# Second attention of a fused block: scaled float16 pairs in place of float32 operands

## What is computed

```python
q = jnp.einsum('btm,mhd->bthd', x, w_aq)
k = jnp.einsum('btm,mhd->bthd', x, w_ak)
v = jnp.einsum('btm,mhd->bthd', x, w_av)
q = _rope(q)
k = _rope(k)
s = jnp.einsum('bihd,bjhd->bhij', q, k) / D_HEAD
...
s = s - jnp.asarray(INF_APPROX, x.dtype) * mask
p = jax.nn.softmax(s, axis=-1)
o = jnp.einsum('bhij,bjhd->bihd', p, v)
r = jnp.einsum('bihd,hdm->bim', o, w_ao)
```

## Time and profile before

| | |
|---|---|
| median of 3 runs | 2135.99 us (2134.03 to 2136.79) |
| the profiled execution | 2136.71 us, its span 2134.9 us |
| attention A's loop | from 58 us, 1212 us long |
| attention B's loop | from 1376.7 us, 711.6 us long |
| mean granted clock of TensorE | 0.978 |

### The profile page before, as it was taken

One profiled execution on the slowest core, in us unless ns is written; L12 is line 12 of the kernel. 1 busy time (PEld: TensorE's weight loads), 2 busy tenths in 40 slices (PEclk: granted clock), 3 DMA queues, 4 the chain that ended last, 5 costly groups with the idle time before them and its releaser, 6 DMA issues.

```text
span 2134.9 us, 51602 instructions
## 1 busy us (share of the span) xinstructions
PE 1976.8 (93%) x21751; PEld 1427.7 (67%) x21751; DVE 1522.4 (71%) x2818; ACT 1478.4 (69%) x1812; POOL 1280.5 (60%) x687
## 2 busy tenths in 40 slices
PE   4899999999999999999999987699999999999997
PEld 3466666656666666666666655478788887878886
DVE  7777777877777777787777756666666766667642
ACT  2788888888888888888888983245555454554563
POOL 5798898898888988988988981222313122131200
PEclk8999999999999999999999998699999999999999
DMA  5100100110110010010011001000000000000000
GB/s 134 31 15 18 31 17 17 32 24 10 32 31 13 20 32 17 17 31 22 14 29 31 2 2 50 1 1 1 1 1 1 1 1 1 1 1 1 1 1 20
DMA packets 45013, 37.67 MB, mean 18 GB/s; under 512 B 8304, under 2 KB 44144, under 8 KB 44528
## 3 DMA queue, kind: packets, MB, share of 16 engines
q1 hardware_dynamic: 43824, 33.60, 6.4%
q10 hardware_dynamic: 960, 0.79, 0.2%
HBM read 8.15 MB, written 1.05 MB: 4 GB/s over the span
## 4 chain that ended last, share of the span: by engine, by line
PE 79%; DVE 16%; issue 2%; ACT 1%; POOL 1%; ACTq 0%; DMA 0%; SPq 0%; DVEq 0%
PE ST L1354 9%; PE ST L1355 9%; PE OO L1491 7%; PE RING L1229 6%; PE OO L1298 5%; PE OO L1300 5%; PE OO L1297 5%; DVE maxes L903 4%; PE RING L1444 3%; PE OO L1229 3%; PE ST L1514 3%; PE ST L1491 3%; PE ST L1518 3%; PE ST L1516 3%; PE RING L1424 3%
## 5 line engine op out<-in xcount | busy, mean ns | idle before, releaser
L517 POOL TENSOR_TENSOR PAB<-PR,PAB 128x1024 f16<-128x1024 f32 x342 | 724.2, 2132 | 98.0 <-ACT PAB L655 96.2
L903 DVE TENSOR_REDUCE maxes<-RING 128x1 f32<-128x512 f32 x710 | 468.8, 684 | 148.3 <-PE RING L1229 147.8
L655 ACT ACTIVATE PAB<-ST,exp_scale 128x1024 f16<-128x1024 f32 x512 | 567.2, 1108 | 0.0
L653 ACT ACTIVATE PR<-ST,exp_scale 128x1024 f32<-128x1024 f32 x342 | 381.3, 1115 | 123.6 <-PE ST L1355 120.1
L1297 PE MATMUL OO<-VP,PAB 128*128 128x66 f16 x4096 | 440.4, 193 | 2.8 <-POOL PAB L517 2.8
L1298 PE MATMUL OO<-VP,PAB 128*128 128x64 f16 x4096 | 441.0, 194 | 0.0
L1300 PE MATMUL OO<-VP,PAB 128*128 128x66 f16 x4096 | 438.7, 192 | 0.0
L1297 PEld LDWEIGHTS OO<-VP,PAB 128*128 128x128 f16 x4096 | 379.6, 96 | 73.0 <-issue 15.7
L1298 PEld LDWEIGHTS OO<-VP,PAB 128*128 128x128 f16 x4096 | 376.9, 97 | 60.2
L1354 PE MATMUL ST<-QL,KH 128*128 128x512 f16 x1024 | 388.5, 379 | 2.3 <-ACT PAB L655 1.4
L517 POOL TENSOR_TENSOR PAB<-VF,PAB 128x1024 f16<-128x1024 f32 x170 | 362.5, 2132 | 44.4 <-ACT PAB L655 43.3
(11 more groups left out here) (202 smaller groups left out, 3260.8 us busy)
## 6 DMA issues: line engine op xcount, KB each, us to landing
KH<-HS SPq DMA_DIRECT2D x120, 64.0 KB, 2.0
QL<-HS SPq DMA_DIRECT2D x64, 64.0 KB, 2.0
QL<-LS SPq DMA_DIRECT2D x64, 64.0 KB, 2.0
QH<-HS SPq DMA_DIRECT2D x64, 64.0 KB, 2.0
KL<-LS SPq DMA_DIRECT2D x60, 64.0 KB, 2.0
X<-in_L_attn_a_x SPq DMA_DIRECT2D x4, 256.0 KB, 4.8
SHARED<-in_rope_cos SPq DMA_DIRECT2D x1, 1024.0 KB, 4.8
SHARED<-in_rope_sin SPq DMA_DIRECT2D x1, 1024.0 KB, 7.6
```

Of the source, the lines that this page charges most:

```text
L517: pool.tensor_tensor(PB[:, s, :], PRA[g % PR_SLOTS], PA[:, s, :], ALU.subtract).then_inc(p_low_ready, 1)
L653: act.activation(PRA[g % PR_SLOTS], ST[step % 2][:, :], ACT.Exp, scale=scale)
L655: act.activation(PA[:, step % SLOTS_A, :], ST[step % 2][:, :], ACT.Exp, scale=scale).then_inc(sa.exps, 1)
L903: dve.reduce_max(maxes[:, i // BLOCKS, i % BLOCKS:i % BLOCKS + 1], bank[:, :], X_AXIS).then_inc(sa.ring_taken, 1)
```

## The change

Attention B gets float16 pairs throughout.

- **Weights.** During attention A ACT squares the weights of B, DVE sums them, one product totals them (ring item `total`), and DVE makes a power of two of each head's Q, K and V from the exponent. POOL multiplies the weights by it in 12 pieces, ACT writes the high halves (WHB) and POOL the low halves (WLB).
- **x.** XNT is replaced by XH and XL: ACT writes the high part of a transposed block, DVE the low part.
- **Projections and values.** Each is three products (high·high, low·high, high·low). ACT writes the high part of V and DVE the low part. V is laid out as two columns of ones, 128 high, 128 low.
- **Scores.** Four products add up: `row_units` (4 rows of 2^15) times MROW (the scaled negative maximum of each query, one row for each query tile), then the three products of K and Q in float16; on the diagonal the mask product too. `spread`, its copy, the priming and the fill go, and scores(g) waits for the exps of step g - 2 alone.
- **P.** ACT takes exp twice from PSUM: into float32 (PRB, three slots) and into float16 (PAH, four slots). POOL subtracts (PAL). P·V of step g is three products a query tile and follows the scores of step g + 2.
- **Order.** Projections and values sit at other steps. POOL does the rope sum one step after the projection and the low part of Q or K four steps after; ACT does the high part three steps after. DVE normalises a unit at step 2 of the next. The first two score steps stand ahead of the eight maxima of the second unit.

```diff
+LAG_B = 2
+SLOTS_B = 4
+PR_SLOTS_B = 3
+PIECES_B = 12
...
-VALUES_B = {(2, 4): 0, (2, 7): 1, (2, 10): 2, (3, 9): 3}
-PROJECT_B = {(1, 5): [0], (2, 3): [1], (2, 6): [2], (2, 9): [3], (3, 1): [4], (3, 3): [5], (3, 5): [6], (3, 8): [7]}
+VALUES_B = {(2, 1): 0, (2, 11): 1, (3, 9): 2, (3, 12): 3}
+PROJECT_B = {(1, 1): [0], (1, 4): [1], (1, 7): [2], (2, 3): [3], (2, 6): [4], (2, 9): [5], (3, 1): [6], (3, 5): [7]}
...
-    if step == steps_b(qb) - 3 and (next_qb or next_head):
-        items += [("spread", next_qb)]
...
+                i = u - UNITS_A
+                if 0 <= i < PIECES_B and step == 0:
+                    pool.wait_ge(b_scaled, 1)
+                    wait(pool, wb_high, i - 1)
+                    pool.tensor_tensor(wb_tmp[:, i % 2, :, :],
+                                       RAW[:, i * 2 * DB:(i + 1) * 2 * DB].rearrange("p (a c) -> p a c", c=DB),
+                                       b_up[:, 2 * i:2 * i + 2].unsqueeze(2).broadcast_to((P, 2, DB)), ALU.mult
+                                       ).then_inc(wb_put, 1)
+                if 0 <= i < PIECES_B and step == 4:
+                    pool.wait_ge(wb_high, i + 1)
+                    pool.tensor_tensor(piece_b(WLB, i), wb_tmp[:, i % 2, :, :], piece_b(WHB, i), ALU.subtract
+                                       ).then_inc(wb_low, 1)
...
-                high, low = ((QH, QL), (KH, KL))[j % 2]
+                high, low = ((QH16, QL16), (KH16, KL16))[j % 2]
                 pool.wait_ge(sbb.high_ready, index + 1)
-                pool.tensor_tensor(low[hs][:, q], F[:, j % 2, :], high[hs][:, q].bitcast(F32),
-                                   ALU.subtract).then_inc(sbb.operands_ready, 1)
+                pool.tensor_tensor(low[hs][:, q], F[:, j % 2, :], high[hs][:, q], ALU.subtract
+                                   ).then_inc(sbb.operands_ready, 1)
 
...
+            for g, (it, ul, step) in enumerate(PLACES_B):
+                c0 = max(0, step - BT * (ul % BLOCKS)) * P
+                pool.wait_ge(sbb.exps, g + 1)
+                wait(pool, sbb.pv, g - SLOTS_B + 1)
+                pool.tensor_tensor(PAL[:, g % SLOTS_B, c0:BLK], PRB[g % PR_SLOTS_B][:, c0:BLK],
+                                   PAH[:, g % SLOTS_B, c0:BLK], ALU.subtract).then_inc(p_low_ready_b, 1)
+                for head, n, j in projects_before(g, 1):
+                    rope_sum_b(j, n)
+                for head, n, j in projects_before(g, 4):
+                    low_b((head + 1) % 2, j, (head + 1) * 2 * BLOCKS + j)
 
...
                                ).then_inc(sa.exps, 1)
+                if u == 1 and step in (1, 3, 5):
+                    act.wait_ge(bweights, 48)
+                    part = slice(step // 2 * 8 * DB, (step // 2 + 1) * 8 * DB)
+                    act.activation(PBUF[:, part], RAW[:, part], ACT.Square, scale=float(np.sqrt(D))
+                                   ).then_inc(b_squared, 1)
+                i = u - UNITS_A
+                if 0 <= i < PIECES_B and step == 2:
+                    act.wait_ge(wb_put, i + 1)
+                    act.activation(piece_b(WHB, i), wb_tmp[:, i % 2, :, :], ACT.Copy).then_inc(wb_high, 1)
...
+            for g, (it, ul, step) in enumerate(PLACES_B):
+                hs, qb = divmod(ul, BLOCKS)
+                head = it * 2 + hs
+                c0 = max(0, step - BT * qb) * P
+                scale = exp_scale_b[:, head:head + 1]
+                wait(act, p_low_ready_b, g - PR_SLOTS_B + 1)
+                act.wait_ge(sbb.scores, g + 1)
+                act.activation(PRB[g % PR_SLOTS_B][:, c0:BLK], SB[g % 2][:, c0:BLK], ACT.Exp, scale=scale)
+                wait(act, sbb.pv, g - SLOTS_B + 1)
+                act.activation(PAH[:, g % SLOTS_B, c0:BLK], SB[g % 2][:, c0:BLK], ACT.Exp, scale=scale
+                               ).then_inc(sbb.exps, 1)
+                for n, item in ITEMS_B[g]:
+                    if item[0] == "values":
+                        values_high_b(1 - hs, item[1], RING[n % 2], n)
+                for phead, n, j in projects_before(g, 3):
...
                 q = slice(b * BLK, (b + 1) * BLK)
-                dve.tensor_tensor(XL[:, q], O[b % 2][:, :], XH[:, q], ALU.subtract).then_inc(xnt_ready, 1)
+                dve.tensor_tensor(XL[:, q], bank[:, :], XH[:, q], ALU.subtract).then_inc(xnt_ready, 1)
 
...
-                    link(dve.tensor_copy(negparts[:, 0:BT].bitcast(F32R), negmax[:, :]))
-                    dve.tensor_tensor(negparts[:, BT:AUX], negmax[:, :], negparts[:, 0:BT],
-                                      ALU.subtract).then_inc(s.max_ready, 1)
+                    dve.tensor_scalar(negparts[:, :], negmax[:, :], 1.0 / ROW_UNIT, lifts_b[:, head:head + 1],
...
+            def take_values_b(hs, part, bank, item, count):
+
+                dve.wait_ge(vb_high, count)
+                v = VBS[:, hs, part * BT:(part + 1) * BT, :]
+                dve.tensor_tensor(v[:, :, V2B_AT:VB], bank[:, :].rearrange("p (t c) -> p t c", c=DB),
+                                  v[:, :, V1B_AT:V2B_AT], ALU.subtract).then_inc(sbb.ring_taken, 1)
...
+            for g, (it, ul, step) in enumerate(PLACES_B):
+                hs, qb = divmod(ul, BLOCKS)
+                head = it * 2 + hs
+                if step == LAG_B and g > step:
+                    normalise_b((ul - 1) % UNITS_B, g - step)
...
-            def project_b(hs, j, bank, item, head):
+            def project_b(j, bank, item, head):
 
                 claim(sbb, item)
-                pe.wait_ge(sbb.wst_ready, head + 1)
-                blk = j // 2
-                pe.matmul(bank[:, :], WST[:, hs, (j % 2) * DB:(j % 2 + 1) * DB], XNT[:, blk * BLK:(blk + 1) * BLK],
-                          start=True, stop=True).then_inc(sbb.ring_put, 1)
-
-            def values_b(hs, part, bank, item, head):
+                pe.wait_ge(wb_low, PIECES_B)
+                q = slice(j // 2 * BLK, (j // 2 + 1) * BLK)
+                w = slice(j % 2 * DB, (j % 2 + 1) * DB)
+                pe.matmul(bank[:, :], WHB[:, head, w], XH[:, q], start=True, stop=False)
+                pe.matmul(bank[:, :], WLB[:, head, w], XH[:, q], start=False, stop=False)
...
+            def scores_b(g):
+
+                it, ul, step = PLACES_B[g]
+                hs, qb = divmod(ul, BLOCKS)
+                if step == 0:
+                    pe.wait_ge(sbb.ring_taken, ROWS_OF_B[it * UNITS_B + ul] + 1)
+                wait(pe, sbb.exps, g - 1)
+                keys = slice(step * P, (step + 1) * P)
+                c0 = max(0, step - BT * qb) * P
+                q = slice(qb * BLK + c0, (qb + 1) * BLK)
+                tile = SB[g % 2][:, c0:BLK]
+                pe.matmul(tile, row_units[:, :], MROW[:, qb % 2, c0:BLK], start=True, stop=False,
+                          skip_group_check=True)
+                if step >= BT * qb:
+                    pe.matmul(SB[g % 2][:, c0:c0 + P], mask_ident[:, :], later_keys_t[:, :], start=False,
+                              stop=False, skip_group_check=True)
+                pe.matmul(tile, KH16[hs][:, keys], QH16[hs][:, q], start=False, stop=False, skip_group_check=True)
+                pe.matmul(tile, KL16[hs][:, keys], QH16[hs][:, q], start=False, stop=False, skip_group_check=True)
+                pe.matmul(tile, KH16[hs][:, keys], QL16[hs][:, q], start=False, stop=True, skip_group_check=True
+                          ).then_inc(sbb.scores, 1)
+
...
+            def pv_b(g, half):
...
-                    pe.wait_ge(sbb.exps, g + 1)
+                    if step == 0:
+                        pe.wait_ge(sbb.ring_taken, VALUES_OF_B[it * 2 + hs] + 1)
+                        wait(pe, sbb.o_taken, it * UNITS_B + ul - 1)
+                    pe.wait_ge(p_low_ready_b, g + 1)
+                v = VBS[:, hs, step, :]
                 for qt in range(max(2 * half, step - BT * qb), 2 * half + 2):
-                    bank, at = (OB[ul % 2][0], qt * VB) if qt < 3 else (OB[ul % 2][1], 0)
-                    ins = pe.matmul(bank[:, at:at + VB], PRB[:, step % 2, qt * P:(qt + 1) * P],
-                                    VBS[:, ul // BLOCKS, step, :], start=(step == 0 and qt in (0, 3)),
-                                    stop=(step == BT * qb + qt), skip_group_check=True)
+                    bank, at = (OB[ul % 2][0], qt * V2B_AT) if qt < 3 else (OB[ul % 2][1], 0)
+                    o = bank[:, at:at + V2B_AT]
+                    tile = slice(qt * P, (qt + 1) * P)
+                    high, low = PAH[:, g % SLOTS_B, tile], PAL[:, g % SLOTS_B, tile]
+                    pe.matmul(o, high, v[:, 0:V2B_AT], start=(step == 0 and qt in (0, 3)), stop=False,
+                              skip_group_check=True)
+                    pe.matmul(o[:, V1B_AT:V2B_AT], high, v[:, V2B_AT:VB], start=False, stop=False,
+                              skip_group_check=True)
+                    ins = pe.matmul(o, low, v[:, 0:V2B_AT], start=False, stop=(step == BT * qb + qt),
...
+            for g, (it, ul, step) in enumerate(PLACES_B):
...
```

(16 more changed lines are left out.)

518 lines of the change are left out of this document (230 added, 288 removed).

## The result

| | before | after |
|---|---|---|
| median of 4 runs, us | 2136.4 (2134.0 to 2136.8) | 2230.6 (2229.4 to 2232.1) |
| profiled span, us | 2134.9 | 2229.6 |
| first attention, first score product to end | 58.5 to 1269.3 | 61.3 to 1284.4 |
| second attention's loop | 711.6 | 792.5 |
| a head of it | 91.1 | 99.9 to 103.1 |

The account below looks back on a forecast made before the run. PE was taken to bound the second attention. Heads of 76.5 + 7 = 83.5 us made its loop 650, 61.5 less; with +5, -0.5, -2.5 and +0.5 that is -59 from 2136.0: 2077 us, range 2042 to 2112.

Parts of the forecast that it names:

- PE's work a head, 76.5: Second attention: PE's products, priced by columns, sum to 75.4 us a head; 76.5 taken, 10.7 less than before.
- Waits, 7 (4 to 12): Second attention: PE's new waits a head; those listed come to 10 us, 7 taken, 4 and 12 as bounds.
- The maximum behind a projection: Block rows 1 and 2: PE reaches maxima behind DVE's projections too early, by 0.85, 0.5, 0.85 and 0.4 us.
- The turn: Block rows 1 to 3: PE waits at the turn for DVE, 1.4, 1.3 and 1.7 us.
- (f): Scaled negative maximum on DVE takes 0.23 to 1.59 us; PE waits 0.4 at the rows product; worst case 38 over the stage.
- POOL (e): Second attention: a rope sum or low part on POOL delays P's low part, needed for P·V; 1.3 us a head.
- First attention, +5 (0 to +12): First attention: added ACT, POOL and DVE work on the weights costs 5 us, between 0 and 12.
- between -2.5: Between the attentions: spread, priming and first fill go, low parts of X come; -2.5 us, between +3 and -6.
- A: Second attention: waits stay at 4 us a head as in the first; head 80.5, time 2048; chance 0.24.
- B: Second attention: P's low part comes late from POOL, 9.7 us more waits a head; 2110 (2103 to 2122); chance 0.15.
- C: Second attention: every projection's 2.07 us on DVE is exposed, 16.6 a head; time 2144; chance 0.08.
- D: Second attention: each 130-column P·V instruction holds PE for 0.10 us, 18 more a head; time 2221; chance 0.03.

Follow-up runs that it names:

- e1_rows128: The changed kernel with 128 rows, 124 of them zeros, instead of 4 in the product that brings the maximum in; 2177.4 us.
- e10_new_places_rows4: The kernel with the best order found (e5_new_places), with the 4-row product put back; 2124.1 us against 2062.7.
- e5_new_places: The changed kernel with the 128-row product, the output's own wait, and projections, values, turn, output, rope sums and high parts at other steps; 2062.7 us.
- e4_output_own_wait: The 128-row kernel with turn and output one step later in rows 1 to 3, its output waiting only for its turned tile's copy; 2124.5 us.
- e9_rows64: The changed kernel with 64 rows instead of 4 in the product that brings the maximum in; 2220.9 us, one run.
- e3_old_places: The 128-row kernel (e1_rows128) with values and projections at the steps of the kernel before; 2162.4 us.
- e8: e5_new_places with three-operand scaled maximum, later start fills, sums and exponent arithmetic spread over units, GpSimd's weight pieces at step 4; 2048.3 us.

## Why the prediction was wrong, step by step

The prediction is off by 154 us. Two terms of its sum failed. "Four float16 products (three pairs and the new product of rows) cost 4 x 7.36 = 29.5 us" priced the product of rows by its columns; it costs 61 us more. And "A head takes 76.5 + 7 = 83.5" had the waits too small and gave no price to what comes with them: with 128 rows and the order unchanged (e1_rows128) a head takes 95.0, 11.5 over my 83.5, some 90 us over the loop. Either would have spoiled the forecast: without the first the kernel still takes 2177, and without the second it takes 2124 (e10_new_places_rows4). By its own steps:

- **PE's work a head, 76.5: right but for one term.** In e5_new_places, at a clock of 1.00 and with 128 rows, PE works for 76.6 (my 1.5% on top of the 75.4 is an allowance that no run takes apart). Float16 P·V at 0.057, scores at 0.216, the diagonal, the projections: each as priced. The failed term is that of the scores, four products at one price: the fourth has four rows and costs 0.192 more a step, 7.7 a head, 61.4 in all. I had the evidence and did not use it: the four spreads of 512 columns that the change removes stand in my sum at "some 1.5", 0.38 each where columns give 0.22. They have 8 rows. Two rows of the kernel before, PE's timeline in its second attention:

```profile
1465.28 0.49 PE L1473 MATMUL RING<-MROW,ones_r 8*128 8x512 f32 x1
1465.70 0.71 PE L1491 MATMUL OO<-PAB,PR 128*128 128x129 f32 x4
```

  The successor starts 0.42 behind the 8-row product, 0.20 later than its columns ask for. (That its rows cost this, and not its format, wasn't tested.) I took that price away with the spreads, four a head, and did not put it on the 40 products of rows that come.
- **Waits, 7 (4 to 12): 10.9 by the waits view, inside the bounds, but not the waits I listed; 13.5, outside them, once the rows cost nothing (e1_rows128).** The maximum behind a projection: 2.6 forecast, 3.0 seen. The turn: 1.4, 1.3 and 1.7 forecast, 2.6 seen. The rows product (f): 0.4 forecast, 1.35 seen (12.7 over the loop, where my worst case was 38). POOL (e): 1.3 forecast, none seen for P·V; POOL's lateness shows at DVE instead, 3.7 once a head, for the buffer F, and some 1.4 of it at PE, within the 3.0 at maxima. Not in my list at all: the output, 3.2. I had costed the moved places and not the order of items within a step nor the argument of the wait that the diff drops; e4_output_own_wait puts that wait, with what came along, at 31 us.
- **What a wait costs.** From e1_rows128 to e5_new_places the order alone takes 115 us away. A head in the middle of the loop falls by 17.1, from 95.0 to 77.85, and the waits in it by 12.4, from 13.5 to 1.1. The rest has two parts. First, a wait breaks PE's stream: the product ahead of it shows its whole length, 0.38 where the next one would start after 0.22 in a stream, or 0.22 where it would start after 0.06. So each wait takes some 0.16 that the view doesn't count; 12 waits more a head make 1.9, an estimate. Second, the clock: heads of one kernel that wait alike take 98.4 at 1.00 and 99.95 at 0.98 (e9_rows64), and 91.4 and 92.9 (e3_old_places). That is 1.5 us for 0.02, and 2.8 are left for the 0.96 of e1_rows128. I had named a lower clock as a way to be wrong, but put no price on it. The two heads of the changed kernel, 100.7 on average, are 84.5 of work (e10_new_places_rows4), 10.9 of waits, 1.7 of breaks, 2.4 of clock (against the 98.4 of e9_rows64), and 1.2 that I can't place.
- **First attention, +5 (0 to +12): 12.3.** The mechanism was right, the size just over its upper bound, which I had named as a sign of being wrong. Units 8 to 19 cost 6.8 (e8 takes it back by placing, so the operations fit but not at step 0), and unit 3 costs 6.0.
- **Start -0.5, between -2.5, end +0.5: +2.8, -1.6, +0.3.** The end is right in size. The stretch between looks right by luck: the eight maxima moved across its mark, and like for like it is +5.8, over my bound of +3. What makes it longer no run takes apart.
- **Rivals.** A (waits stay at 4): refuted for this order; with a better one they are 1.1. B (low part of P late): refuted as the main releaser. P·V has no such wait in the two heads and one of 0.5 a head in e1_rows128; but POOL's lateness is real and costs PE some 1.4 a head through F. C (every projection exposed, 16.6 a head): only a third is there, 5.3 a head of waits on a projection's last operation, 3.0 at maxima and 2.3 at the output. D (P·V instructions at 0.10): refuted, they stand 0.057 apart with a weight load each; the 81 ns of the Trainium skill (TensorE: Matmul & The Clock Gate, back-to-back issue gap) do not hold for this stream. D had the right idea in the wrong place: one instruction in each step has a price above its columns.
- **The sum.** From my loop of 650 to the 792.5 measured: 61 for the rows, 31 for 3.9 more waits a head, 14 for their breaks, 19 for the clock, 7 for the eight maxima behind the mark, and some 10 that I can't place. Taken away instead of added up: in e5_new_places, with 128 rows and waits of 1 in place of 7, the loop is 622.9, 27 below my 650. Seven heads of 77.85 account for 40 less; what is beside them comes to 12 more than my 65.6, and 7 of that is the maxima. Three slips in the prediction's arithmetic change little: waits of 12 give 2112 and not 2103, the last head comes to 65.1 and not 65.6, and the listed waits to 8.7 and not 10 if (f) is met once.

The Trainium skill has the rule that I needed. TensorEngine Tiling (Array Packing), Key Properties, says that a change of the tiling mode drains TensorE, and Available Configurations lists 64-row and 32-row modes beside the full one. I did not weigh it, because nothing here is packed. The trace agrees in each point that it can show: 4, 32 and 64 rows cost the same, 128 nothing more than its columns, and the cost lies on both sides of the product, 0.09 and 0.10. That the engine changes mode and drains is the page's reading; the runs show only the gaps. Another page of the Trainium skill (TensorE: Matmul & The Clock Gate, Why this matters for your kernels) has a single product of 32 rows take the time of one with 128. No run here has such a product alone; between full products it takes 0.19 more.

## What to carry to other kernels

Give every matmul of a dense stream all 128 rows, with zeros if need be: a few rows save nothing and cost 0.19 us each time (61 us here, of the 74 that the change wins in e5_new_places). Price a product by its distance to both neighbours in a trace, not by its columns, and look for an odd shape in the rows you have. In a ring of two buffers the order of items within a step and the exact count of each wait are worth as much as the arithmetic: the same operations took 2177 us in one order and 2063 in another. So before a cheaper operation is judged, lay the queues beside each other again.

## What the runs showed of the hardware

- A product of 4 rows between 128-row products costs 0.19 to 0.20 us more than one of 128 rows, on both sides of it: 0.15 and 0.32 around 512 columns, 0.14 and 0.16 around 128. With 32 and 64 rows the gaps around 512 columns are the same.
- Float16 products of 128 and 130 columns with a new weight load each stand 0.057 us apart for as long as 12 in a row.
- In the first attention, where GpSimd is busy for 1085 of 1223 us, a DVE operation on 4 elements takes 0.16 to 1.61 us (median 0.91), in the two-scalar and in the three-operand form alike. Two small ones that stood beside a GpSimd operation ended with it, the longer after 2.08; in a pause of GpSimd such operations took 0.16 to 0.17.
- A wait of PE costs some 0.16 us more than the waits view counts (an estimate from lengths of 0.38 against starts 0.22 apart).
- With 10 to 12 us of waits in a head of 100, none over 2.3, the granted clock is 0.93 to 0.98 in the changed kernel, and 0.97 to 1.00 in e9_rows64 with the same waits; a head takes 1.5 us more at 0.98 than at 1.00. With 1 us of waits it is 1.00 for six heads in a row.
